# Spreading routing weights over partitions: by matmul or by transfers from memory

## The chip, the cores and the metric

The kernel is written in Bass, by hand, for one core of one Trainium2 chip. Five engines run their own instruction streams side by side and wait for each other by semaphores: TensorE (PE) for matmuls and transposes, VectorE (DVE), ScalarE (ACT), GpSimd (POOL) and SyncE (SP). SP issues nearly all DMA transfers; 16 DMA engines carry them out. The metric is the device time of one execution in microseconds.

## The reference

Two layers work on 8 x 256 tokens of 256 numbers. Each has a norm, an attention, a norm and a set of experts, and each adds its result to x. The change concerns the first set of experts, which is:

```python
scores = sigmoid(x @ router_w.T)                    # 2048 tokens x 16 experts
_, topk_idx = top_k(scores + e_bias, 4)
topk_w = take_along_axis(scores, topk_idx, axis=1)
topk_w = topk_w / (topk_w.sum(axis=1) + 1e-20)
combine = zeros((T, 16)).at[arange(T)[:, None], topk_idx].add(topk_w)
for gu_w, d_w, c in zip(gate_up_proj, down_proj, combine.T):   # 16 experts, 96 hidden each
    g, u = split(x @ gu_w.T, 2, axis=1)
    routed = routed + c[:, None] * (silu(g) * u @ d_w.T)
shared = silu(x @ shared_gate_w.T) * (x @ shared_up_w.T) @ shared_down_w.T
```

All 16 experts are computed for all tokens, and the weight of an expert is zero for a token that did not choose it. The second layer has a cross attention over 64 context rows and 8 experts of 704 hidden rows, of which each token takes two.

## The kernel before

**The first experts as one wide layer.** The 16 experts with 96 hidden rows each stand side by side as 1536 hidden rows, in 12 chunks of 128; a 13th chunk, of 96 rows, is the shared expert. So a chunk holds rows of two experts, and the routing weight must be there per hidden row (partition) and token (column). The 2048 tokens are 16 tiles of 128, in 4 groups of 4 tiles (NG = 4), so that a chunk's hidden values for a group are a tile of 128 x 512.

**One cycle.** For each group `g` and each chunk `c` (0 is the shared one, `chunk_of` gives the place of the others), TensorE does `up0` (gate and up, each 2 halves of the 256 inputs, each as three matmuls of high and low parts: 12 matmuls of 512 columns, into banks 0 to 3 of PSUM) and `down0` (4 tiles of tokens, three matmuls each of 256 columns, into banks 6 and 7). ACT makes silu of the gate (L837). DVE multiplies it with the up half (L1713, "product"), multiplies with the routing weights (L1718), makes the high part (a cast, L1723) and the low part in two halves (a subtraction, L1727, `h_low`), for which `down0` waits. TensorE's order in `ffn0_group` is: `up0` of chunk c+1, then `down0` of chunk c.

**How the weights come to the partitions.** DVE chooses the experts of the first four tiles before the first cycle, and those of the other twelve in pieces in the first group's cycles (`select_rest`). It splits the weights in three bfloat16 parts (`c3`, 96 columns). TensorE turns them (`turn_weights`, L1182), ACT copies them into `cT` (L828), and for each chunk one bfloat16 matmul (L1161) with a matrix of ones and zeros, `spread`, puts the chunk's weights for 512 tokens into bank 4 of PSUM, from which L1718 reads them. GpSimd makes `spread` at the start of the kernel (L544, L548).

**What runs beside it.** GpSimd makes low parts: first of the inputs and of the first experts' weights (L558, L566, L572), then of the second experts' weights. Those, 68 parts of 128 x 512, are loaded by SP (L427), copied to a high part by ACT (L855), subtracted by GpSimd (L604, two instructions a part) and stored again by SP as high and low part (L436, L438). `parts_by` deals them out: 11 in the first group, from its fifth chunk on, and 19 in each later one, that is two in the chunks 2, 4, 6, 8, 10 and 12 and one in the others. ACT handles them behind the cycle's silu. GpSimd waits for the choice of the first four tiles (`pool.wait_ge(b_c3, 3)`) before it goes on with the low parts of the inputs.

In the groups 1 to 3, DVE also makes the statistics of the next norm (chunks 1 and 3) and its rows (chunks 5 and 7, L1472).

## Time and profile before

| | |
|---|---|
| median of 3 runs | 739.35 us (735.06 to 740.98) |
| the profiled execution's own time | 740.54 us |
| its span, first to last instruction | 738.8 us |
| mean granted TensorE clock | 0.941 |
| TensorE busy | 694.2 us, 94% of the span |
| VectorE busy | 471.8 us, 64% |
| ScalarE busy | 257.4 us, 35% |
| GpSimd busy | 356.1 us, 48% |
| moved by DMA | 114.96 MB, mean 156 GB/s |

The profile is of one execution. All times of its rows are in microseconds from the first instruction; "busy" is the time in which at least one instruction of the engine runs. The time outside the span is 1.7 us. A matmul's duration includes the way through the array, so matmuls overlap and their starts tell what each costs.

### The profile page before, as it was taken

The page shows a single profiled execution, that of the slowest core. Times are in us where ns is not written, and L with a number is a line of the kernel's source. Part 1 is how long each engine was busy: PE and PEld are TensorE (multiplying, and loading weights), DVE is VectorE, ACT ScalarE, POOL GpSimd, SP SyncE. Part 2 cuts the span into 40 slices and gives each one's busy share as a digit, 9 for nine tenths or more (in the row PEclk, how much of TensorE's full clock was granted, in tenths as well). Part 3 has the DMA queues.
Part 4 walks back from the last instruction along what each step waited for, and adds up shares of the span by engine and source line. Part 5 has one row for each costly group of instructions (what it writes and reads, how often), then busy time and mean ns, then how long its engine had stood idle before and what let it go on. Part 6 is the DMA issues. An engine that isn't in the chain of part 4 may idle for free.

```text
span 738.8 us, 14867 instructions
## 1 busy us (share of the span) xinstructions
PE 694.2 (94%) x4707; PEld 622.9 (84%) x4707; DVE 471.8 (64%) x1331; ACT 257.4 (35%) x484; POOL 356.1 (48%) x435
## 2 busy tenths in 40 slices
PE   4899999999999999998999984899999999999996
PEld 3758878888888888886677773799999999999995
DVE  4958597677777777775799958344544454454443
ACT  1355512333333333346466622222222232323221
POOL 6217693455446545549222034255354655465553
PEclk9786599999999999999899985899999999999999
DMA  9900103678877787769900047422425445434222
GB/s 220 343 3 1 58 0 122 236 247 271 264 242 257 262 265 248 248 230 430 367 20 31 31 138 267 147 44 41 154 45 151 97 122 155 151 75 135 44 37 22
DMA packets 60266, 114.96 MB, mean 156 GB/s; under 512 B 15185, under 2 KB 29394, under 8 KB 57778
## 3 DMA queue, kind: packets, MB, share of 16 engines
q1 hardware_dynamic: 50514, 103.48, 41.0%
q0 software_dynamic: 8736, 10.39, 8.5%
q8 instruction: 37, 0.61, 0.3%
q10 hardware_dynamic: 960, 0.33, 0.2%
q14 instruction: 19, 0.16, 0.1%
HBM read 68.89 MB, written 45.29 MB: 155 GB/s over the span
## 4 chain that ended last, share of the span: by engine, by line
PE 84%; DVE 10%; issue 3%; ACT 2%; DMA 1%; POOLq 0%; POOL 0%; DVEq 0%
PE ps L1114 19%; PE ps L1115 19%; PE ps L1116 19%; PE ps L1399 4%; PE ps L1244 2%; PE ps L1253 2%; PE ps L986 2%; PE ps L1290 2%; PE ps L1050 2%; PE ps L1041 2%; PE ps L1161 1%; PE ps L1266 1%; PE ps L1201 1%; PE ps L1378 1%; PE ps L1282 1%
## 5 line engine op out<-in xcount | busy, mean ns | idle before, releaser
L604 POOL TENSOR_TENSOR part_lo<-wexp,part_hi 128x256 fp32r<-128x256 f32 x136 | 104.8, 795 | 107.4 <-ACT part_hi L855 106.6
L715 POOL DMA_INDIRECT out_rows<-vbd,slot_row x39 | 63.3, 1623 | 105.6 <-DVE vbd L1947 74.0
L1114 PE MATMUL ps<-w_hi,x_high 128*128 x312 | 104.6, 335 | 1.1 <-DVE x_low L1952 1.1
L1115 PE MATMUL ps<-up_low,x_high 128*128 x312 | 101.1, 324 | 0.0
L1116 PE MATMUL ps<-w_hi,x_low 128*128 x312 | 101.0, 324 | 0.0
L1968 DVE TENSOR_TENSOR arena<-arena,ps 128x704 f32<-128x704 f32 x39 | 34.6, 888 | 102.5 <-ACT arena L954 102.5
L1114 PE MATMUL ps<-xn_high,gu_high 128*128 (+3 forms) x208 | 90.9, 437 | 0.0
L837 ACT ACTIVATE wexp<-ps 128x512 f32<-128x512 f32 (+1 forms) x52 | 31.1, 599 | 147.1 <-PE ps L1116 147.1
L1115 PE MATMUL ps<-xn_low,gu_high 128*128 (+3 forms) x208 | 81.9, 394 | 0.0
L1116 PE MATMUL ps<-xn_high,gu_low 128*128 (+3 forms) x208 | 81.7, 393 | 0.0
L954 ACT ACTIVATE arena<-ps 128x704 f32<-128x704 f32 x39 | 29.6, 760 | 119.1 <-PE ps L1116 119.1
L538 POOL TENSOR_TENSOR rstd<-ve,mhalf 128x2 f32<-128x2 f32 (+1 forms) x31 | 23.3, 751 | 91.7 <-DVE ve L1461 91.7
L1727 DVE TENSOR_TENSOR h_low<-wexp,h_high 128x256 fp32r<-128x256 f32 (+1 forms) x104 | 62.6, 642 | 1.8
L1114 PE MATMUL ps<-dn_high,h_high 128*128 128x256 f32 (+1 forms) x208 | 59.7, 287 | 1.3 <-DVE h_low L1727 1.3
L1114 PEld LDWEIGHTS ps<-w_hi,x_high 128*128 128x128 f32 x312 | 59.3, 190 | 1.5 <-issue 1.5
L1114 PE MATMUL ps<-w_hi,hT_high 128*128 x195 | 58.2, 298 | 2.0 <-DVE hT_high L1961 2.0
L1115 PEld LDWEIGHTS ps<-up_low,x_high 128*128 128x128 f32 x312 | 59.4, 190 | 0.0
L1116 PEld LDWEIGHTS ps<-w_hi,x_low 128*128 128x128 f32 x312 | 59.2, 190 | 0.0
L1115 PE MATMUL ps<-dn_low,h_high 128*128 128x256 f32 (+1 forms) x208 | 58.8, 283 | 0.0
L1116 PE MATMUL ps<-dn_high,h_low 128*128 128x256 f32 (+1 forms) x208 | 58.6, 282 | 0.0
L1116 PE MATMUL ps<-w_hi,hT_low 128*128 x195 | 55.0, 282 | 0.0
L1115 PE MATMUL ps<-down_low,hT_high 128*128 x195 | 55.0, 282 | 0.0
(297 smaller groups left out, 1675.1 us busy)
## 6 DMA issues: line engine op xcount, KB each, us to landing
wexp<-in_wexp SPq DMA_DIRECT2D x68, 256.0 KB, 3.4
w_hi_rows<-part_hi SPq DMA_DIRECT2D x68, 256.0 KB, 3.1
w_lo_rows<-part_lo SPq DMA_DIRECT2D x68, 256.0 KB, 2.7
w_hi<-w_hi_rows SPq DMA_DIRECT2D x8, 2048.0 KB, 19.5
up_low<-w_lo_rows SPq DMA_DIRECT2D x8, 1408.0 KB, 6.0
down_low<-w_lo_rows SPq DMA_DIRECT2D x8, 768.0 KB, 8.3
wexp<-in_gu SPq DMA_DIRECT2D x2, 1632.0 KB, 11.2
xn_rows<-arena SPq DMA_DIRECT2D x8, 256.0 KB, 2.1
```

Of the source, the lines that this page charges most:

```text
L538: pool.tensor_tensor(rstd[:, bass.ds(b * TB, TB)], ve[:, bass.ds(b * TB, TB)], mhalf[:, 0:1].broadcast_to([P, TB]), ALU.pow).then_inc(ln_r ...
L604: r = pool.tensor_tensor(part_lo[:, n % 2, some], part_w[:, n % 4, some], part_hi[:, n % 2, some].bitcast(F32), ALU.subtract)
L715: pool.indirect_dma_start(out=out_rows, out_offset=bass.IndirectOffsetOnAxis(ap=slot_row[:, i:i + 1], axis=0), in_=yb[:, i % 2, :], in_off ...
L837: act.activation(sg0[0:rows, c % 2, :], bank(c % 2)[0:rows, :], ACT.Silu).then_inc(b_silu, 1)
L954: act.activation(sg1.rearrange("p (a n) -> p a n", a=2), bank(0, 2).rearrange("p (a n) -> p a n", a=2)[:, :, 0:HALF1], ACT.Silu).then_inc( ...
L986: mm = pe.transpose(bank(bank_of(norm, k))[:, m * S + j * P:m * S + (j + 1) * P], rows[:, m * P:(m + 1) * P], ident[:, :])
L1114: pe.matmul(out, high, rows_high, start=start, stop=False, skip_group_check=True)
L1115: pe.matmul(out, high, rows_low, start=False, stop=False, skip_group_check=True)
L1116: return pe.matmul(out, low, rows_high, start=False, stop=stop, skip_group_check=True)
L1399: mm = pe.transpose(bank(4, 2)[:, c * P:(c + 1) * P], h1[:, c * P:(c + 1) * P], ident[:, :])
L1727: dve.tensor_tensor(h_low[0:rows_, c % 2, cols], hm0[0:rows_, c % 2, cols], h_high[0:rows_, c % 2, cols].bitcast(F32), ALU.subtract).then_ ...
L1968: dve.tensor_tensor(h1[:, 0:I1].rearrange("p (a n) -> p a n", a=2), sg1.rearrange("p (a n) -> p a n", a=2), bank(2, 2).rearrange("p (a n) ...
```

## The change

The routing weights are no longer spread by TensorE. TensorE turns the float32 weights of a group of tiles (64 rows: 4 tiles x 16 experts) with one transpose per group, ACT copies them, SP stores them into a table in memory (`cw_rows`, 16 experts x 2048 tokens), and for each chunk SP loads the two experts' rows into one of four buffers in SBUF (`w_spread`), each row repeated over its partitions. DVE multiplies with that buffer. The split in three bfloat16 parts, the matrix `spread` and the memset of `c3` go. GpSimd's wait for the choice goes. A few semaphores are merged. The SP queue, which only handled the parts, now runs by group and chunk.

```diff
-        cT = arena[0:96, 0:1024].bitcast(BF16)
-        c3 = arena[:, 1024:1792].bitcast(BF16).rearrange("p (t c) -> p t c", t=NT)
-        spread = arena[0:96, 1792:2560].bitcast(BF16)
+        cT = arena[0:4 * E0, 0:NT // 4 * P]
...
+        w_spread = [view(wexp, at, 512) for at in (20416, 20928, 4096, 4608)]
+        w_in, cw_stored = [sem(f"w_in{n}") for n in range(4)], sem("cw_stored")
+        cw_rows = nc.dram_tensor("cw_rows", (E0, NT * P), F32, kind="Internal").ap()
...
+            def store_weights(first, groups):
+                for j in range(4):
+                    sp.dma_start(cw_v[:, first:first + groups, j, :],
+                                 cT[j * E0:(j + 1) * E0, first * P:(first + groups) * P].rearrange(
+                                     "e (g p) -> e g p", p=P)).then_inc(cw_stored, 16)
+
+            def load_weights(n):
+                g, c = n // (C0 - 1), chunk_of(n % (C0 - 1) + 1)
+                if n >= 4:
+                    sp.wait_ge(b_mult, n - 3)
+                sp.wait_ge(cw_stored, 16 * 8 if g else 16 * 4)
+                e = c * P // I0
+                edge = (e + 1) * I0 - c * P
+                for expert, lo, hi in ((e, 0, edge), (e + 1, edge, P)):
+                    sp.dma_start(w_spread[n % 4][lo:hi, :],
+                                 cw_rows[expert, g * 512:(g + 1) * 512].partition_broadcast(hi - lo)).then_inc(w_in[n % 4], 16)
...
+            sp.wait_ge(b_cT, 1)
+            store_weights(0, 1)
+            sp.wait_ge(x_new, XA)
+            for n in range(3):
+                load_part(n)
+            for n in range(3):
+                load_weights(n)
+            for g in range(NG):
+                for q in range(C0):
+                    if g == 0 and q == 10:
+                        sp.wait_ge(b_cT, 2)
+                        store_weights(1, NG - 1)
+                    n = g * (C0 - 1) + q + 2
+                    if q and n < NG * (C0 - 1):
+                        load_weights(n)
+                    for part in range(parts_by(g, q - 1), parts_by(g, q)):
+                        store_part(part)
...
-            pool.memset(spread, 0.0).then_inc(pool_step, 1)
-            v = spread.rearrange("p (e u) -> p e u", e=E0)
-            for part in range(3):
-                pool.wait_ge(pool_step, 10 + part)
-                pool.affine_select(out=v, in_=v, compare_op=ALU.not_equal, fill=1.0, base=-32 * part,
-                                   pattern=[[-1, E0], [0, I0]], channel_multiplier=1).then_inc(pool_step, 1)
...
-            pool.wait_ge(b_c3, 3)
             for n in range(3, 5):
                 low_rows(n)
...
+            def copy_weights(first, groups):
+                act.wait_ge(b_turned, first + groups)
+                at = slice(first * P, (first + groups) * P)
+                act.activation(cT[:, at], bank(4)[0:4 * E0, at], ACT.Copy).then_inc(b_cT, 1)
+            copy_weights(0, 1)
...
                     act.activation(sg0[0:rows, c % 2, :], bank(c % 2)[0:rows, :], ACT.Silu).then_inc(b_silu, 1)
-                    if k == 0 and c == 0:
-                        copy_weights(0)
                     if k == 0 and c == 9:
-                        copy_weights(1)
-                        copy_weights(2)
-                    if k == 0 and c == 11:
-                        copy_weights(3)
+                        copy_weights(1, NG - 1)
...
-                    if c:
-                        if k == 0 and c == 1:
-                            pe.wait_ge(b_cT, 1)
-                            pe.wait_ge(pool_step, 13)
-                        else:
-                            pe.wait_ge(b_mult, g * (C0 - 1) + c - 1)
-                        pe.matmul(bank(4), spread[:, chunk_of(c) * P:(chunk_of(c) + 1) * P], cT[:, bass.ds(g * 512, 512)],
-                                  start=True, stop=True).then_inc(b_spread, 1)
...
-                for j in range(4):
-                    mm = pe.transpose(at[0:96, j * P:(j + 1) * P], c3[:, 4 * g + j, :], identb[:, :])
-                mm.then_inc(b_turned, 1)
+                pe.wait_ge(b_chosen, 2 if g else 1)
+                pe.transpose(bank(4)[0:4 * E0, g * P:(g + 1) * P], cw0[:, 4 * g:4 * g + 4, :].rearrange("p t e -> p (t e)"),
+                             ident[:, :]).then_inc(b_turned, 1)

             up0(0, 0, 0)
             pe.wait_ge(b_sig, 1)
+            pe.wait_ge(v_ready, B)
+            turn_weights(0)
             ffn0_group(0, 0)
...
                     if c:
-                        dve.wait_ge(b_spread, g * (C0 - 1) + c)
-                        dve.tensor_tensor(hm0[:, c % 2, :], hm0[:, c % 2, :], bank(4), ALU.mult).then_inc(b_mult, 1)
+                        dve.wait_ge(w_in[(c - 1) % 4], g * (32 * (C0 - 1) // 4) + 32 * ((c - 1) // 4 + 1))
+                        dve.tensor_tensor(hm0[:, c % 2, :], hm0[:, c % 2, :], w_spread[(c - 1) % 4], ALU.mult).then_inc(b_mult, 1)
```

Where instructions moved, the two programs' order shows it. First TensorE, between the first chunk's up matmuls (of 96 rows) and the second chunk's; before:

```order
L1114 MATMUL ps<-xn_high,gu_high 96x512
L1115 MATMUL ps<-xn_low,gu_high 96x512
L1116 MATMUL ps<-xn_high,gu_low 96x512
L1114 MATMUL ps<-xn_high,gu_high 128x512
L1115 MATMUL ps<-xn_low,gu_high 128x512
```

and with the change (the three lines of `in_parts` are now L1134 to L1136):

```order
L1134 MATMUL ps<-xn_high,gu_high 96x512
L1135 MATMUL ps<-xn_low,gu_high 96x512
L1136 MATMUL ps<-xn_high,gu_low 96x512
L1186 MATMUL ps<-ident,arena 64x128
L1134 MATMUL ps<-xn_high,gu_high 128x512
L1135 MATMUL ps<-xn_low,gu_high 128x512
```

The transpose of the first weights (L1186), which stood behind the second chunk as four instructions, now stands ahead of it. Next ScalarE, from the sigmoid of the router's scores on; before (L837 is silu, L828 the copy of the turned weights, and a table load belongs to the function behind it):

```order
L824 ACT_TABLE_LOAD
L824 ACTIVATE arena<-ps 128x256
L837 ACT_TABLE_LOAD
L837 ACTIVATE wexp<-ps 96x512
L828 ACTIVATE arena<-ps 96x512
L837 ACTIVATE wexp<-ps 128x512 x5
```

and with the change (L862 is silu, L852 the copy):

```order
L847 ACT_TABLE_LOAD
L847 ACTIVATE arena<-ps 128x256
L852 ACTIVATE arena<-ps 64x128
L862 ACT_TABLE_LOAD
L862 ACTIVATE wexp<-ps 96x512
L862 ACTIVATE wexp<-ps 128x512 x5
```

The copy moved ahead of the first silu and of the load of its table. Last SyncE's queue, behind the first stores of the filler rows; before:

```order
L420 DMA po_rows<-arena 128x8
L427 DMA wexp<-in_wexp 128x512 [waits x_new]
L427 DMA wexp<-in_wexp 128x512 x3
L436 DMA w_hi_rows<-part_hi 128x512 [waits p_hi]
L438 DMA w_lo_rows<-part_lo 128x512 [waits p_lo]
```

and with the change:

```order
L418 DMA po_rows<-arena 128x8
L430 DMA cw_rows<-arena 16x128 [waits b_cT]
L430 DMA cw_rows<-arena 16x128 x3
L425 DMA wexp<-in_wexp 128x512 [waits x_new]
L425 DMA wexp<-in_wexp 128x512 x2
L442 DMA wexp<-cw_rows 96x512 [waits cw_stored]
L442 DMA wexp<-cw_rows 32x512
L442 DMA wexp<-cw_rows 64x512 [waits cw_stored]
```

Four stores into the table and the wait for ACT's copy stand ahead of the first parts, and two loads per chunk (96 and 32 partitions, or 64 and 64) come in between the parts from then on, three chunks ahead of their use.

## Rows read from the trace of the kernel before

**Rows 1.** The page's chain of work that ended last, by engine.

```profile
PE 84%; DVE 10%; issue 3%; ACT 2%; DMA 1%; POOLq 0%; POOL 0%; DVEq 0%
```

**Rows 2.** Busy time by stretch, one group: stretch, length, engines, clock, DMA, GB/s.

```profile
core 0: us, PE busy (x) PEld busy (x) DVE busy (x) ACT busy (x) POOL busy (x), PEclk, DMA share, GB/s
155.00:213.50 58.50, 58.24 (x333) 50.35 (x332) 43.67 (x87) 19.19 (x34) 30.93 (x40) 1.00 0.78 258
```

**Rows 3.** Summaries of single lines: duration ns least/median/most, first and last start.

```profile
L1161 PEld LDWEIGHTS ps<-arena x48: 96/97/98, 97.9 to 323.8; 96*128 96x128 bf16 x48
...
L1718 DVE TENSOR_TENSOR wexp<-wexp,ps x48: 686/689/689, 98.4 to 324.3; 128x512 f32<-128x512 f32 x48
...
L1727 DVE TENSOR_TENSOR h_low<-wexp,h_high x104: 411/426/962, 95.3 to 326.3; 128x256 fp32r<-128x256 f32 x96, 96x256 fp32r<-96x256 f32 x8
```

**Rows 4.** Timeline, TensorE, a spreading matmul and the next: start, length, what.

```profile
206.71 0.39 PE L1161 MATMUL ps<-arena 96*128 x1
206.94 0.47 PE L1114 MATMUL ps<-xn_high,gu_high 128*96 x1
```

**Rows 5.** The start of the kernel: timeline of GpSimd and TensorE, summary of L1499.

```profile
10.29 1.57 POOL L548 TENSOR_SCALAR_AFFINE_SELECT arena<-arena 96x1536 bf16<-96x1536 bf16 x1
...
L1499 DVE TENSOR_SCALAR wexp<-wexp,small x2: 340/870/1399, 10.6 to 11.9; 128x256 f32<-128x256 f32 x2
...
12.42 1.94 PE L997 MATMUL ps<-wexp 128*128 128x64 f32 x8 [4.56 <-DVE wexp L1499]
```

**Rows 6.** Timeline, VectorE, a cycle with two parts (idle before and its releaser in brackets).

```profile
178.79 0.69 DVE L1713 TENSOR_TENSOR wexp<-wexp,ps 128x512 f32<-128x512 f32 x1 [0.68 <-ACT wexp L837]
179.82 0.69 DVE L1718 TENSOR_TENSOR wexp<-wexp,ps 128x512 f32<-128x512 f32 x1 [0.34 <-PE ps L1161]
180.55 0.53 DVE L1723 CAST h_high<-wexp 128x512 fp32r<-128x512 f32 x1
...
181.11 0.84 DVE L1727 TENSOR_TENSOR h_low<-wexp,h_high 128x256 fp32r<-128x256 f32 x1
...
181.87 0.95 DVE L1727 TENSOR_TENSOR h_low<-wexp,h_high 128x256 fp32r<-128x256 f32 x1
```

**Rows 7.** Timeline, GpSimd, three of the four instructions of the same cycle.

```profile
179.36 0.73 POOL L604 TENSOR_TENSOR part_lo<-wexp,part_hi 128x256 fp32r<-128x256 f32 x1 [2.97 <-ACT part_hi L855]
...
180.05 0.74 POOL L604 TENSOR_TENSOR part_lo<-wexp,part_hi 128x256 fp32r<-128x256 f32 x1
...
180.75 0.92 POOL L604 TENSOR_TENSOR part_lo<-wexp,part_hi 128x256 fp32r<-128x256 f32 x1
```

**Rows 8.** Timeline, TensorE, the same chunk's down matmuls, first and second half.

```profile
182.37 0.28 PE L1114 MATMUL ps<-dn_high,h_high 128*128 128x256 f32 x1
...
183.08 0.28 PE L1114 MATMUL ps<-dn_high,h_high 128*128 128x256 f32 x1
```

**Rows 9.** Timeline, an h_low over GpSimd's power of two columns.

```profile
221.65 0.89 POOL L538 TENSOR_TENSOR rstd<-ve,mhalf 128x2 f32<-128x2 f32 x1
...
222.02 0.42 DVE L1727 TENSOR_TENSOR h_low<-wexp,h_high 128x256 fp32r<-128x256 f32 x1
```

**Rows 10.** Timeline, the first microseconds of the first experts, several engines.

```profile
88.97 1.28 ACT L837 ACT_TABLE_LOAD   x1
...
91.56 0.22 DVE L1629 TENSOR_TENSOR arena<-arena,recs 128x64 f32<-128x64 f32 x1
...
92.57 0.40 PE L1116 MATMUL ps<-xn_high,gu_low 128*96 128x512 f32 x1
...
92.84 3.01 POOL L566 TENSOR_TENSOR xn_low<-wexp,xn_high 128x256 fp32r<-128x256 f32 x4 [4.19 <-DVE arena L1658]
...
93.00 0.59 ACT L837 ACTIVATE wexp<-ps 96x512 f32<-96x512 f32 x1 [2.76 <-PE ps L1116]
...
98.44 0.69 DVE L1718 TENSOR_TENSOR wexp<-wexp,ps 128x512 f32<-128x512 f32 x1
```

**Rows 11.** The parts' stores in SP's queue: issue ns, and time to landing.

```profile
L436 SPq DMA_DIRECT2D w_hi_rows<-part_hi x68: 319/320/723, 116.6 to 325.6; - x68
...
DMA to landing us min/median/max: 2.0/3.1/5.5
```

104 lines of the change are left out of this document (32 added, 72 removed).

## The prediction

> **What bounds the kernel now.** I read the chain of work first: TensorE carries 84% of it and VectorE 10% [rows 1]. The table by stretches puts the changed stage in place. In the first experts' stage one group of 512 tokens takes 58.50 us; TensorE is busy in 58.24 of it at the full granted clock, VectorE in 43.67, GpSimd in 30.93, and the DMA engines stand at 0.78 of their time while moving 258 GB/s [rows 2]. So in this stage TensorE sets the end, and VectorE, GpSimd and the DMA engines have slack, but not much. Then the summaries of single lines gave prices [rows 3], and the timelines of single cycles and of the stage's first microseconds showed who waits for whom [rows 4 to 11].
>
> I call one chunk of 128 hidden rows a cycle: 12 matmuls up, 12 down and one spreading matmul.
>
> **The change, step by step.** Times are summed against the profiled execution's own 740.54 us; the median of the three runs is 739.35, 1.19 lower, and I move the result by that at the end.
>
> *1. The spreading matmuls go.* There are 48 [rows 3]. One pushes the next matmul 0.23 us back (206.71 to 206.94) [rows 4]. The first three lie where VectorE, not TensorE, sets the pace (step 4), so 45 count: 45 x 0.23 = -10.4 us. VectorE's wait for them, 0.34 us between the two products of a cycle (179.48 to 179.82) [rows 6], is no gain of its own.
>
> *2. The start of the kernel.* GpSimd no longer makes the spreading matrix. Its last piece runs from 10.29 for 1.57 us, and over it the first of two like VectorE instructions takes 1.40 us, the second 0.34; TensorE begins at 12.42, behind them [rows 5]. TensorE waited for nothing else there, so -1.1 us. If a transfer ends next instead, 0.
>
> *3. The product with the weights moves from PSUM to SBUF.* This is the term I trust least to intuition. The instruction with a PSUM operand takes 686 to 689 ns in all 48 cases, with GpSimd running or not [rows 3]. The instructions with two SBUF inputs (h_low) take 426 ns in the median and up to 962, and the long ones stand over GpSimd's (181.11 with 0.84, over the one from 180.75 to 181.67) [rows 3, 6, 7]. The new product has two SBUF inputs too, w_spread and hm0. Its own length, unheld, no row shows: it lies between 0.43 (256 columns) and 0.85 (twice that), and I keep the 0.69 of the PSUM form with as many columns.
>
> Read off row by row: a VectorE instruction of this kind begins its work 0.14 us before the end of a running GpSimd one (h_low ends at 181.95, 0.42 after 181.53; GpSimd's ends at 181.67), and a GpSimd one that had to wait ends 0.60 after VectorE's end (the cast's at 181.08) [rows 6, 7]. With these two numbers I write out the cycle with two parts, zero being the product's start (178.79). GpSimd's first instruction runs 0.57 to 1.30. The product ends at 0.69; the new one may start at 1.16 and ends at 1.85 (before: 1.72, since it waited 0.34 for TensorE). GpSimd's second ends at 2.45, the cast waits to 2.31 and ends at 2.74 (before 2.29). GpSimd's third ends at 3.34, the first h_low waits to 3.20 and ends at 3.62 (before 3.16); the second ends at about 4.50 (before 4.03). TensorE began the down matmuls at 3.58 and their second half at 4.29 [rows 8]; without the spreading matmul it comes at 3.35 and 4.06. With 0.04 from one engine's end to another's start it waits 0.31, then 0.17 more: 0.48 us, twice what the cycle saves. In a cycle with one part GpSimd has two instructions, and the first h_low ends at 3.20, in time for 3.35, so those cycles keep the whole 0.23.
>
> There are 6 two-part cycles in each of the three later groups and 3 in the first, 21 in all: 21 x 0.48 = +10.1 us. A GpSimd instruction on two columns does not hold VectorE (h_low at 222.02 takes 0.42 over the power from 221.65) [rows 9]; those on 256 columns do. The lower end is 0 (GpSimd off VectorE's instructions); the upper +13.7, if besides the twelve cycles in which VectorE also makes statistics or rows of the next norm lose 0.3 each, a first h_low's wait.
>
> The Trainium skill is stricter, in "SBUF — State Buffer", § Who interferes with whom: of a VectorE instruction with two SBUF inputs and a GpSimd one that reads SBUF, whoever issues second is blocked until the first has finished. With each wait 0.14 us longer for it, and three of them ahead of the first h_low, the term would be about 21 x 0.9 = +19 and the sum +10. The rows show the release 0.14 before the end [rows 6, 7], so the measured number goes into the sum and the rule's case is counted with rival C.
>
> *4. The first weights.* This path is new. Before, the choice's last step kept by the change ends at 91.78, TensorE issues the first chunk's matmuls until 92.8, and transposes and copy come behind the second chunk and the first silu [rows 10]. Now the transpose stands before the second chunk's up matmuls, and ACT copies before its first silu. Three things are late: the choice itself, since GpSimd now runs over it instead of waiting until 92.84 [rows 10], by 0 to 2.5 us (five short instructions with two inputs, up to 0.5 each; I take 1.5); the silu, since its table load (1.28 us, hidden at 88.97 today) [rows 10] now stands behind the copy; and the table's round trip. With the choice at 93.3 the copy ends at 94.1, the table load at 95.4, silu at 96.0, 2.4 later than before (93.59). In that time the four stores issue (0.32 each as the parts' stores, landing from 2.0 later [rows 11]), then the three part loads and the first weights, 0.4 each, landing 3.1 later as a store does in the median: 94.1 + 1.3 + 2.0 + 0.8 + 3.1 = 101.3. VectorE reaches the first such product at 98.44 [rows 10] + 2.4 = 100.8, so the load is the later one: some 2.9 us late. GpSimd is done with its pieces 4.19 us earlier, which frees a VectorE instruction or two of the second and third chunk (0.4 us each). I take +2.5, between +0.5 (choice not slowed, table load hidden) and +5 (all of it, and a landing of 5.5 us).
>
> *5. Edits at nothing.* Sixteen bfloat16 transposes become four of float32 (a few tenths either way). The merged semaphores wait for the same events. The DVE instructions removed in the rest of the choice lay in VectorE's slack of 14 us in 58.5 [rows 2]. The part loads wait for the first copy now, but the parts' first store is at 116.6 us [rows 11].
>
> *6. The queue and the DMA engines.* SP's queue takes two more issues in each cycle (0.64 us at 0.32), ahead of the parts' loads and stores. Traffic in one group: 19 parts of three transfers of 256 KB, 14.9 MB; the weights add 12 x 256 KB = 3.1 MB. At 258 GB/s the share is 0.78, so full use would be 330 GB/s [rows 2]. 18.1 MB in the 55.8 us that TensorE would leave are 324 GB/s, 0.98 of it. I price it at 0, because a late part has most of a cycle before it holds ACT's next silu. If that cover is gone it is rival B.
>
> Sum: -10.4 - 1.1 + 10.1 + 2.5 + 0 = +1.1. 740.54 + 1.1 = 741.6 profiled, 740.4 as a median: no change.
>
> **Rivals.** *A: GpSimd and VectorE do not get in each other's way*, because GpSimd drifts off VectorE's instructions. For it: the product no longer waits 0.34 us; against: the 0.84 and 0.95 [rows 6]. Then term 3 is about 0.5: -10.4 - 1.1 + 0.5 + 2.5 = -8.5, 731 us.
>
> *B: the DMA engines become the bound*, the side on which it is slower. A weight row is read 32 to 96 times from one place in memory, which no transfer of this size in the trace does. If such a load takes twice the time of a plain one, a group needs (14.9 + 6.3) MB at 330 GB/s = 64.2 us, against 58.5 today: +5.7 in each of three groups, +17.1, and in the rest -2.1 (spreading) + 1.4 (contention) - 1.1 + 2.5 = +0.7: 757 us. At 1.4 times it is 58.5 and 740. It decides from about 1.6 times (746.7). For it: share 0.78 already, landings of up to 5.5 us against 2.0 at the least [rows 11]. Against: a row of 2 KB, once read, may be quick to read again.
>
> The Trainium skill gives about 358 GB/s of memory bandwidth for a core ("DMA: Bandwidth & Descriptors", § Specifications); by that 324 GB/s would fit, and rival B would need the repeated reads.
>
> *C: GpSimd's wait was the point.* Choice slowed by 2.5 and every cycle with statistics late as well: the upper ends of terms 3 and 4 together, -11.5 + 13.7 + 5 = +7.2, 746.6 us, the edge of 1%.
>
> **Numbers.** A change under 1% (7.4 us) is about what a measurement of this kernel can't tell from none. The forecast with C: 0.50, its own range 733 to 746.6. A: 0.17. B: 0.33, most of it between 747 and 765. So faster 0.17, same 0.50, slower 0.33, and a range of 729 to 760.
>
> **What would show it.** Right: product rows of the new line at 0.69 where GpSimd rests and about 1.1 where it runs; a group of 57 to 59 us with TensorE waiting for h_low in the two-part cycles; silu first at 95 to 96; TensorE's first matmul behind VectorE at 11.4. Wrong: TensorE never idle and 55.5 us a group (A); ACT or VectorE waiting for transfers, landings over 4.5 us and a DMA share near 1 (B).

## The result, and the profile after

The changed kernel takes 745.16 us in the median of 15 executions (740.95 to 748.9), the kernel before 738.15 us in 15 beside them (731.87 to 740.98). The ratio is 1.0103, with a 95% interval of 1.0073 to 1.0133: slower by about 1%, 7 us. The forecast was 740.4 us in 729 to 760. The time lies in the range, 4.8 us above the value; whether the change is under 1% the interval can't tell, as it holds that bound. Some executions of the kernels edited for the experiments lie 12 us or more above the others of their kernel, so what is compared between profiles is above all groups 1 to 3, where the granted clock is 0.99 to 1.00.

The profiled execution of the changed kernel has a time of 740.95 us, almost that of before (740.54), and still the kernel is 7 us slower. The two differ in TensorE's granted clock ahead of the first experts. These are windows of both kernels (length, busy time with count of TensorE, its weight loads, VectorE, ScalarE and GpSimd, then the granted clock, the DMA share and GB/s); first before:

```profile
61.20:88.40 27.20, 27.20 (x114) 24.47 (x113) 17.48 (x61) 14.85 (x22) 19.93 (x29) 0.50 0.12 39
```

and after:

```profile
61.20:79.20 18.00, 15.58 (x100) 14.03 (x99) 15.28 (x54) 12.71 (x19) 13.79 (x20) 0.81 0.00 0
```

Half the full clock (1.2 instead of 2.4 GHz) stood there for 27 us in the one, and mostly the full clock in the other. Both kernels have executions of both kinds. Of the changed kernel's 15, those at a mean clock of 0.962 and more take 741 to 742 us (6 of 7), those at 0.955 and less 746 to 749; before's take 732 to 733 at 0.966 and more, and mostly 737 to 742 at 0.957 and less. So profiles are comparable only at the same clock. A second profile of the changed kernel (experiment 1) has before's clock there, and the account below uses it. These are four stretches: from TensorE's first matmul to the first experts, the first group (to its first addition to x), groups 1 to 3, the rest; before:

```profile
12.42:88.37 75.95, 72.64 (x311) 59.45 (x311) 55.96 (x294) 37.10 (x77) 34.79 (x50) 0.71 0.35 111
88.37:153.00 64.63, 64.09 (x355) 53.74 (x356) 50.43 (x135) 18.55 (x32) 34.91 (x46) 0.97 0.38 126
153.00:329.09 176.09, 175.30 (x999) 151.55 (x998) 132.28 (x259) 58.91 (x106) 92.11 (x120) 1.00 0.76 252
329.09:738.80 409.71, 380.21 (x3039) 356.58 (x3037) 229.52 (x626) 141.55 (x269) 184.08 (x192) 0.95 0.42 124
```

and after, the second profile:

```profile
11.37:87.31 75.94, 72.73 (x311) 59.52 (x311) 55.26 (x293) 37.07 (x77) 34.80 (x50) 0.71 0.32 100
87.31:154.08 66.77, 62.68 (x331) 52.28 (x332) 51.50 (x126) 16.83 (x29) 35.73 (x45) 0.95 0.60 181
154.08:334.12 180.04, 172.55 (x963) 144.27 (x962) 134.92 (x259) 61.53 (x107) 91.99 (x121) 1.00 0.91 300
334.12:744.98 410.86, 380.69 (x3039) 356.75 (x3037) 229.60 (x626) 141.51 (x269) 184.19 (x193) 0.95 0.43 124
```

TensorE starts 1.05 us earlier, the first group takes 2.14 us more, groups 1 to 3 take 3.95 more, the rest 1.15 more: +6.2 in all. TensorE's busy time in groups 1 to 3 fell by 2.75 us, but the stretch grew: the engine waits. In the first profile of the changed kernel these groups took 181.78, +5.7. At the higher clock the two kernels' times lie some 9 us apart (741 to 742 against 732 to 733); before has no profile there, so this account doesn't cover the difference. In the changed kernel's first profile the first group took 70.81 us against 66.77 in the second.

Who waits is to be seen at ScalarE. These are its waits in groups 1 to 3 (total, times, longest), before:

```profile
ACT wexp L837 <- PE ps L1116: 106.4, 38, 3.8
ACT part_hi L855 <- issue: 1.7, 2, 1.1
```

and after (first profile; L862 is silu, L875 the copy of a part's high part):

```profile
ACT part_hi L875 <- issue: 63.5, 29, 3.9
ACT part_hi L875 <- DMA w_hi_rows<-part_hi: 40.6, 20, 2.7
ACT wexp L862 <- PE ps L1136: 13.4, 9, 3.9
```

ScalarE used to wait for TensorE's up matmuls ahead of each silu. Now it stands for 104 us at the part's copy. The list puts 63.5 us of that down to "issue", but the trace's landing times settle it: in all 49 cases the copy starts 0.07 us after the store from two parts earlier has landed, which frees the buffer that the copy writes (there are two), and its own part's load had landed at least 2.6 us before. The silu behind it is then late. One such place, a cycle with two parts from ScalarE's timeline in the first of the three groups:

```profile
186.65 0.63 ACT L875 ACTIVATE part_hi<-wexp 128x512 fp32r<-128x512 f32 x1 [0.94 <-issue]
189.99 0.63 ACT L875 ACTIVATE part_hi<-wexp 128x512 fp32r<-128x512 f32 x1 [2.70 <-DMA w_hi_rows<-part_hi]
190.53 0.58 ACT L862 ACTIVATE wexp<-ps 128x512 f32<-128x512 f32 x1
```

The transfers themselves land later; median from issue to landing in groups 1 to 3, before and then after:

```profile
w_hi_rows<-part_hi SPq DMA_DIRECT2D x56, 256.0 KB, 3.2
wexp<-in_wexp SPq DMA_DIRECT2D x53, 256.0 KB, 3.5
```

```profile
w_hi_rows<-part_hi SPq DMA_DIRECT2D x57, 256.0 KB, 4.9
wexp<-in_wexp SPq DMA_DIRECT2D x53, 256.0 KB, 5.1
wexp<-cw_rows SPq DMA_DIRECT2D x22, 192.0 KB, 4.4
```

Where the chain of before was 84% TensorE [rows 1], that of after holds transfers:

```profile
PE 56%; DMA 16%; DVE 13%; issue 6%; SPq 4%; ACT 3%; POOL 2%; POOLq 0%; DVEq 0%; ACTq 0%
```

### The profile page after: what moved, and what is told of

It reads as the page before. It is cut to its first block, busy times and chain, and to the rows that moved or that the text cites. A ratio compares the mean times of both kernels' runs of the same rounds, so it can differ in the third digit from the quotient of the medians.

```text
span 739.2 us, 14870 instructions
## 1 busy us (share of the span) xinstructions
PE 681.0 (92%) x4647; PEld 606.6 (82%) x4647; DVE 479.2 (65%) x1322; ACT 258.2 (35%) x482; POOL 354.8 (48%) x431
## 4 chain that ended last, share of the span: by engine, by line
PE 56%; DMA 16%; DVE 13%; issue 6%; SPq 4%; ACT 3%; POOL 2%; POOLq 0%; DVEq 0%; ACTq 0%
DMA w_hi_rows<-part_hi 13%; PE ps L1134 11%; PE ps L1135 11%; PE ps L1136 11%; PE ps L1404 3%; PE ps L1249 2%; PE ps L1258 2%; PE ps L1295 2%; POOL part_lo L627 2%; DVE wexp L1700 2%; SPq L442 1%; SPq L425 1%; PE ps L1206 1%; ACT part_hi L875 1%; PE ps L1383 1%
## 5 line engine op out<-in xcount | busy, mean ns | idle before, releaser
L627 POOL TENSOR_TENSOR part_lo<-wexp,part_hi 128x256 fp32r<-128x256 f32 x136 | 109.0, 823 | 114.9 <-ACT part_hi L875 102.0
L1134 PE MATMUL ps<-w_hi,x_high 128*128 x312 | 104.7, 336 | 1.1 <-DVE x_low L1934 1.1
L1136 PE MATMUL ps<-w_hi,x_low 128*128 x312 | 101.2, 324 | 0.0
L1134 PE MATMUL ps<-xn_high,gu_high 128*128 (+3 forms) x208 | 84.2, 405 | 3.3 <-DVE wexp L1695 3.3
L875 ACT ACTIVATE part_hi<-wexp 128x512 fp32r<-128x512 f32 x68 | 42.7, 630 | 114.3 <-issue 65.1
L1136 PE MATMUL ps<-xn_high,gu_low 128*128 (+3 forms) x208 | 82.1, 394 | 0.0
L1134 PE MATMUL ps<-dn_high,h_high 128*128 128x256 f32 (+1 forms) x208 | 62.9, 302 | 11.5 <-DVE h_low L1709 11.5
L1695 DVE TENSOR_TENSOR wexp<-wexp,ps 128x512 f32<-128x512 f32 (+1 forms) x52 | 35.6, 684 | 43.3 <-ACT wexp L862 43.2
L1134 PEld LDWEIGHTS ps<-w_hi,x_high 128*128 128x128 f32 x312 | 59.4, 190 | 1.5 <-issue 1.5
L1709 DVE TENSOR_TENSOR h_low<-wexp,h_high 128x256 fp32r<-128x256 f32 (+1 forms) x104 | 59.2, 609 | 1.8
L1134 PEld LDWEIGHTS ps<-dn_high,h_high 128*128 128x128 f32 (+1 forms) x208 | 39.8, 192 | 25.0 <-DVE h_low L1709 19.0
L1134 PE MATMUL ps<-w_hi,hT_high 128*128 x195 | 58.2, 298 | 2.0 <-DVE hT_high L1943 2.0
L1136 PEld LDWEIGHTS ps<-w_hi,x_low 128*128 128x128 f32 x312 | 59.3, 190 | 0.0
L1136 PE MATMUL ps<-dn_high,h_low 128*128 128x256 f32 (+1 forms) x208 | 59.2, 285 | 0.0
```

The costliest lines, as they stand in the source:

```text
L627: r = pool.tensor_tensor(part_lo[:, n % 2, some], part_w[:, n % 4, some], part_hi[:, n % 2, some].bitcast(F32), ALU.subtract)
L875: act.activation(part_hi[:, n % 2, :], part_w[:, n % 4, :], ACT.Copy).then_inc(p_hi, 1)
L1134: pe.matmul(out, high, rows_high, start=start, stop=False, skip_group_check=True)
L1136: return pe.matmul(out, low, rows_high, start=False, stop=stop, skip_group_check=True)
L1695: dve.tensor_tensor(hm0[0:rows_, c % 2, :], sg0[0:rows_, c % 2, :], bank(2 + c % 2)[0:rows_, :], ALU.mult).then_inc(b_prod, 1)
L1709: dve.tensor_tensor(h_low[0:rows_, c % 2, cols], hm0[0:rows_, c % 2, cols], h_high[0:rows_, c % 2, cols].bitcast(F32), ALU.subtract).then_ ...
```

## The experiments

The theories: **the transfers** (landings hold ScalarE, as above), **the shared path** (VectorE's product, now with two SBUF inputs, and GpSimd hold each other), and **GpSimd's missing wait**. An edit that leaves the weights out changes what the second layer computes on, so most are judged by the stretches of their profiles, which the table gives for all (us). DMA share, landing and copy waits are those of groups 1 to 3: the landing is the median of the part loads, and the copy waits are the time in all that ScalarE stood at the copies of the high parts.

| | first group | groups 1 to 3 | DMA share | landing | copy waits |
|---|---|---|---|---|---|
| before | 64.63 | 176.09 | 0.76 | 3.5 | 1.7 |
| changed, first profile | 70.81 | 181.78 | 0.89 | 5.1 | 104.1 |
| changed again | 66.77 | 180.04 | 0.91 | 5.1 | 110.2 |
| no loads | 66.77 | 176.74 | 0.77 | 3.6 | 6.7 |
| product from PSUM | 67.48 | 179.53 | 0.90 | 4.9 | 108.4 |
| both | 77.76 | 169.49 | 0.80 | 3.5 | 4.1 |
| plain loads | 68.40 | 171.89 | 0.94 | 4.2 | 65.7 |
| one row repeated, input tensor | 85.06 | 179.50 | 0.88 | 5.1 | 104.3 |
| 8 copies | 86.77 | 183.95 | 0.87 | 4.8 | 106.8 |
| one row a load | 82.59 | 176.91 | 0.77 | 3.2 | 6.5 |
| first product in PSUM | 66.45 | 181.72 | 0.88 | 5.2 | 109.2 |
| wait back | 67.75 | 181.85 | 0.88 | 5.1 | 110.4 |
| candidate | 80.18 | 171.99 | 0.88 | 4.6 | 22.8 |
| second candidate | 66.97 | 169.35 | 0.89 | 4.8 | 60.6 |

### 1. The changed kernel again

> The changed kernel once more, unedited, beside the others on one chip. The 15 times of it so far lie at 741 to 749, none near 758. If the missing wait can shut VectorE out in this kernel too, some execution shows about 17 us more than the others (755 to 765); if it never does in some 10 executions, what was seen belongs to the edited kernels. The two groups of times (741 to 742 and 745 to 749) should show again, with mean clocks of about 0.965 and 0.945, if they come from how long the clock is low ahead of the first experts (10.2 or 30.7 us).

Four executions: 746.71, 746.29, 760.78 and 744.82 us. The low kind of clock showed as expected (0.939 to 0.955; none of the four had the high one). And one execution of the unedited kernel took some 15 us more than the others; experiment 5 says what that probably is. Four executions are fewer than the ten that the expectation asked for.

### 2. Loads or shared path

No loads:

```diff
-                    if q and n < NG * (C0 - 1):
+                    if q and n < 4:
...
-                        dve.wait_ge(w_in[(c - 1) % 4], g * (32 * (C0 - 1) // 4) + 32 * ((c - 1) // 4 + 1))
+                        dve.wait_ge(w_in[(c - 1) % 4], 32)
```

> The changed kernel, but only the first 4 of the 48 weight loads are issued; VectorE multiplies with whatever stands in the four buffers, so the routing weights of all later products are wrong ones. The product's two SBUF inputs, and GpSimd, are unchanged. DMA theory (late landings hold ACT's copy of the high part, and with it the next silu): the DMA share of groups 1 to 3 falls from 0.89 to about 0.8, landings go back to about 3.4 us for the part loads, a group falls from 60.6 us to 56 to 57, the time by some 10 to 13 us, to 732 to 735. Contention theory (VectorE and GpSimd hold each other over the new product): groups stay at 60 or more and the time at 743 or more. The prediction's own sizes (contention 0.48 us in two-part cycles, DMA nothing) would leave the groups where they are too.

Product from PSUM (bank 4 is filled once, by one matmul more):

```diff
+            pe.matmul(bank(4), gu_high[:, 0, 0:P], xn_high[:, 0, 0:512], start=True, stop=True)
...
-                        dve.tensor_tensor(hm0[:, c % 2, :], hm0[:, c % 2, :], w_spread[(c - 1) % 4], ALU.mult).then_inc(b_mult, 1)
+                        dve.tensor_tensor(hm0[:, c % 2, :], hm0[:, c % 2, :], bank(4) if k else w_spread[(c - 1) % 4], ALU.mult).then_inc(b_mult, 1)
```

> The changed kernel with all its loads, but in groups 1 to 3 VectorE multiplies with bank 4 of PSUM as the kernel before did, which here holds other numbers, so the weights are left out of the result; it still waits for each load. One matmul more fills bank 4 at the start (0.23 us). Contention theory: the product is back to 0.69 in every cycle, groups fall from 60.6 to about 57, the time to 734 to 737. DMA theory: groups stay at 60 to 60.5 with the DMA share at 0.89, the time at 743 to 745.

Both edits:

> Both edits together: 4 loads only, and the product from PSUM in groups 1 to 3 (the routing weights are left out of the result). Neither cause is left, so both theories expect TensorE to be the bound again: a group of 58.5 - 12 x 0.23 = 55.7 us, and 3 x 4.9 = 14.7 us off the changed kernel's time, 730 us. If it is longer than 57 us a group, a third cause is there (TensorE waiting for something else).

Measured, groups 1 to 3: 176.74 without loads, 179.53 with the product from PSUM, 169.49 with both. The times were 734.98 to 760.01 (4 executions), 743.51 in the median of 10 and 737.18 of 6; the profiles carry the verdict. From 169.49 on, where neither cause is left, the shared path alone adds 7.25 us and the loads alone 10.0; together they add 10.6 to 12.3, not 17. So neither theory alone holds: without loads its own theory expected 168 to 171 us and the other 180 and more; with the product from PSUM the shared path's theory expected about 171 and the transfers' 180 to 181.5. Both causes are real, and they overlap; that h_low comes late by the longer of the two delays rather than by their sum fits this and isn't shown. Without loads ScalarE waits for TensorE again (98.8 us), and VectorE's new product (groups 1 to 3: shortest/median/longest, ns) shows the shared path at its full size, no loads first, then the changed kernel:

```profile
L1700 DVE TENSOR_TENSOR wexp<-wexp x36: 691/1122/1281, 158.3 to 326.1; 128x512 f32<-128x512 f32 x36
```

```profile
L1700 DVE TENSOR_TENSOR wexp<-wexp x36: 691/816/1136, 155.1 to 327.1; 128x512 f32<-128x512 f32 x36
```

For "both" I expected 55.7 us a group, and over 57 if a third cause was there. It is 56.5, so none is needed.

### 3. What of the loads: the queue, the bytes, the repeated row

One row a load:

```diff
+                    hi = lo + 1 if n >= 4 else hi
                     sp.dma_start(w_spread[n % 4][lo:hi, :],
```

> The changed kernel with all its 96 issues of weight loads and all their waits, but from the fifth product on each moves one row of 2 KB and not 32 to 96 (the other partitions keep old weights, so the result is not the reference's). It parts the bytes from the queue. If the bytes (the DMA engines' time) make the part loads and stores late: groups 1 to 3 together fall from about 181 us to about 176.7, as with no loads, and the part loads land in 3.5 us again. If SP's queue does it (0.8 us of issuing per cycle, and waits on VectorE ahead of the parts' stores): they stay at 180 to 182, with landings near 3.5 us but the parts still late.

Two executions took 755.12 and 752.77 us, the profiled one with the stall of experiment 5. All issues and waits of SP's queue are there and the groups take 176.91 us, as without loads, with ScalarE at the parts' copies for 6.5 us. So it is what the loads move, and not their issues in SP's queue.

Plain rows, and then one repeated row, both from the second experts' weights:

```diff
-                                 cw_rows[expert, g * 512:(g + 1) * 512].partition_broadcast(hi - lo)).then_inc(w_in[n % 4], 16)
+                                 w_flat[lo:hi, n * 512:(n + 1) * 512]).then_inc(w_in[n % 4], 16)
```

> The changed kernel, but each weight load reads as many plain rows of 2 KB of the second experts' weights, one per partition, and not one row repeated over 32 to 96 partitions (so the routing weights are left out of the result). Same number of transfers, same bytes into SBUF. If the repeated read is what makes the loads dear (the prediction's rival B), their landing falls below 4.2 us and the groups from 60.6 to 58 or less. If it is the plain number of bytes and packets, nothing changes: 60 to 61 us a group, the time within 2 us of the changed kernel's; more memory traffic from distinct addresses could even make it a little longer.

```diff
-                                 cw_rows[expert, g * 512:(g + 1) * 512].partition_broadcast(hi - lo)).then_inc(w_in[n % 4], 16)
+                                 w_flat[expert, n * 512:(n + 1) * 512].partition_broadcast(hi - lo)).then_inc(w_in[n % 4], 16)
```

> As the experiment with plain loads, from the same input tensor, but one row repeated over the 32 to 96 partitions, as the changed kernel repeats its table's (so the routing weights are left out of the result). If repeating a row is what delays: groups 1 to 3 together at about 180 to 182 us and landings of 4.2 us, as in the changed kernel. If the tensor's place matters and not the repeating: 171 to 174 us and landings of 3.5 us, as with plain rows.

The pair differs only in whether the partitions read different rows or the same one. Groups 1 to 3 of the plain rows, then of the repeated row:

```profile
147.77:319.66 171.89, 169.35 (x963) 144.76 (x962) 138.34 (x260) 62.99 (x109) 100.02 (x122) 1.00 0.94 314
```

```profile
172.32:351.82 179.50, 172.66 (x963) 144.38 (x962) 135.52 (x259) 61.68 (x107) 93.73 (x120) 1.00 0.88 300
```

and the landings of parts and of weight loads in the same order:

```profile
wexp<-in_wexp SPq DMA_DIRECT2D x54, 256.0 KB, 4.2
wexp<-in_wexp SPq DMA_DIRECT2D x22, 192.0 KB, 3.9
```

```profile
wexp<-in_wexp SPq DMA_DIRECT2D x54, 256.0 KB, 5.1
wexp<-in_wexp SPq DMA_DIRECT2D x22, 192.0 KB, 4.3
```

Repeating the row costs 7.6 us in three groups. It does not cost the engines' time: share times length is 0.94 x 171.89 = 161.6 us for plain rows, 0.88 x 179.50 = 158.0 for the repeated one and 0.89 x 181.78 = 161.8 for the changed kernel, all with 54 MB. What grows is the time until a transfer, and the others beside it, have landed. So bytes as such did not cost either: as many from different rows leave the groups below those without loads. Executions at a clock of 0.963 to 0.964 point the same way: 731.35 and 733.03 us with plain rows, 738.36 with the repeated one (each of the two kernels also had one or two of over 750, experiment 5).

That plain loads (171.89) beat no loads at all (176.74) neither theory expected. VectorE's product is shorter with them (800 against 1122 ns in the median), so the loads seem to shift GpSimd's work off VectorE's; that it is this shift is argued from the durations, not shown.

The Trainium skill ("DMA: Bandwidth & Descriptors", § Latency and other measured facts) gives a memory access 0.2 us on average and 2 us at high load. From before to the changed kernel the trace agrees in direction: part loads land in 5.1 us at a DMA share of 0.89 to 0.91, in 3.5 at 0.76. Between plain and repeated rows it doesn't go by the share: 4.2 us at 0.94 against 5.1 at 0.88. That the load on one place in memory is what does it, no run here shows.

Eight copies of the table, so that neighbouring partitions read different addresses:

```diff
-                    sp.dma_start(w_spread[n % 4][lo:hi, :],
-                                 cw_rows[expert, g * 512:(g + 1) * 512].partition_broadcast(hi - lo)).then_inc(w_in[n % 4], 16)
+                    sp.dma_start(w_spread[n % 4][lo:hi, :],
+                                 cw_rows[:, expert, g * 512:(g + 1) * 512].unsqueeze(0).broadcast_to(
+                                     [(hi - lo) // 8, 8, 512])).then_inc(w_in[n % 4], 16)
...
```

> The changed kernel with the table in memory kept in 8 copies, 132 KB apart (a row of 2048 tokens and 2 KB of padding, 16 of them), and the repeated rows of a load dealt out over the 8 copies, so that neighbouring partitions read different addresses. Bytes and transfers of the loads are the same; only the stores of the table grow (16 of 128 rows of 512 B where 8 of 16 to 48 stood). Repeated-address theory: the loads' median landing falls from 4.25 to about 3.5 us, groups 1 to 3 together from 181.8 to 172 to 174 us, as with plain rows (171.9). If 8 addresses are still too few: somewhere between 174 and 180. Plain-load-of-another-tensor theory (the loads of e4 were fast because of where they read, not because the rows differ): 180 to 182.

The copies are in fact 160 KB apart (16 rows of 10 KB); the 132 KB in the expectation is my slip. Groups 1 to 3 took 183.95 us, the four times were 755.3 to 769.83: no gain. It is inconclusive on the address, because these transfers also took 0.6 to 0.8 us to issue instead of 0.4, and because their outermost dimension has 4 to 12 steps instead of 32 to 96, with an effect that isn't known. Why a repeated row lands late stays open.

### 4. The shared path, for itself

```diff
-                    dve.tensor_tensor(hm0[0:rows_, c % 2, :], sg0[0:rows_, c % 2, :], bank(2 + c % 2)[0:rows_, :],
+                    dve.tensor_tensor(bank(4) if c else hm0[0:rows_, 0, :], sg0[0:rows_, c % 2, :], bank(2 + c % 2)[0:rows_, :],
                                      ALU.mult).then_inc(b_prod, 1)
...
-                        dve.tensor_tensor(hm0[:, c % 2, :], hm0[:, c % 2, :], w_spread[(c - 1) % 4], ALU.mult).then_inc(b_mult, 1)
+                        dve.tensor_tensor(hm0[:, c % 2, :], bank(4), w_spread[(c - 1) % 4], ALU.mult).then_inc(b_mult, 1)
```

> The changed kernel, but VectorE writes its first product (silu times up) to bank 4 of PSUM for the chunks 1 to 12 and the product with the weights reads it there, so this has one SBUF input instead of two; the transposes of the weights go to bank 5. All loads stay. Contention theory: the product falls from 0.82 to 0.69 or so in the median and its longest from 1.18 to under 0.8; groups 1 to 3 together fall from 181.8 to about 179.5, what the product from PSUM gave with all loads. If one SBUF input is enough to be held by GpSimd, the product stays at 0.8 to 1.2 and the groups at 181 to 183.

```profile
L1701 DVE TENSOR_TENSOR wexp<-ps,wexp x36: 691/691/694, 159.2 to 330.6; 128x512 f32<-128x512 f32 x36
```

With one SBUF input the product is never held: 691 ns in the median and 694 at most, with all loads and GpSimd running. Yet groups 1 to 3 stayed at 181.72 us (743.4 us in the median of 4), with ScalarE at its copies for 109.2: what the product gave back was lost in waiting for the silu. The expected 179.5 was wrong by that. The Trainium skill ("SBUF — State Buffer", § Who interferes with whom) says that a VectorE instruction with at most one SBUF input does not contend with GpSimd; the trace agrees, with 694 against 1136 ns.

### 5. GpSimd's missing wait

The profile of "both" took 77.76 us for its first group. The reason is one VectorE instruction, the first of the choice:

```profile
88.10 14.81 DVE L1617 TENSOR_TENSOR arena<-arena,ebias 128x64 f32<-128x64 f32 x1 [3.48 <-ACT arena L847]
```

It adds 128 x 64 numbers with both inputs in SBUF and takes 0.50 us in the changed kernel's first profile. GpSimd meanwhile, in the same execution:

```profile
87.73 2.80 POOL L590 TENSOR_TENSOR xn_low<-wexp,xn_high 128x256 fp32r<-128x256 f32 x4
90.49 2.12 POOL L582 TENSOR_TENSOR gu_low<-wexp,gu_high 128x256 fp32r<-128x256 f32 x3
...
98.70 4.13 POOL L590 TENSOR_TENSOR xn_low<-wexp,xn_high 128x256 fp32r<-128x256 f32 x6
```

22 instructions without a pause from 87.73 to 102.83, and VectorE's ends at 102.91. It got no turn between them: it was shut out until GpSimd had nothing left. The profiles with 8 copies, one row and the repeated row show the same (14.81, 15.22 and 14.79 us; each time it ends 0.09 us behind the last of 22 instructions of GpSimd, as here), and it is most of what makes their first groups 82.6 to 86.8 us long. In the other profiles without the wait the same instruction took 0.42 to 0.50 us over the same row of GpSimd's. In the kernel before it can't last: GpSimd has its own wait there, for the very choice that VectorE is making, and stands from 88.65 to 92.84 [rows 10]. With that wait put back in the changed kernel:

```diff
             gate_low(5)
+            pool.wait_ge(b_chosen, 1)
             for n in range(3, 5):
```

> The changed kernel with GpSimd's wait for the choice put back where it was, ahead of the low parts of the fourth pair of tiles (pool.wait_ge(b_chosen, 1)); nothing else differs. Theory that the missing wait lets GpSimd, which then has some 19 us of work without a pause, shut VectorE out of the choice: no execution with an instruction of VectorE of over 10 us, and no time near 755 to 760; the choice takes 2.8 instead of 3.95 us and the first group about 1 us less. Rival, that the long instruction came from something else (the edits of that experiment): times near 758 turn up here too, and in the unchanged copy sent along none or as many.

Its times were 743.84, 738.8, 749.55 and 738.18 us. The choice took 2.98 us instead of 3.88 in the kernel run again, about as expected, but the first group took 67.75 us and not 66.77 less 1, at the same clock of 0.95 in that stretch, and groups 1 to 3 took 181.85 against 180.04: that miss stays unexplained. At a clock of 0.962 and more, 738.2 and 738.8 stand against six of the changed kernel's at 741 to 742; two executions and a profile that shows no gain don't make these 3 us a finding. None of the 22 executions of the three kernels with the wait was 15 us above the rest of its kernel, and no VectorE instruction in their profiles exceeds 1.3 us. Of the 19 of the changed kernel itself one was (760.78); it was not the profiled one, so that it had this cause is likely and not shown. In the edited kernels without the wait it was 12 or more of 36, by a profile or by a time some 15 us above the others of its kernel. When it strikes and when not isn't known. With one case in 19, the four executions of the changed kernel with the wait can't show that the wait prevents it; with it GpSimd has no such row of work over the choice, and that is the argument.

The same page and section of the Trainium skill call the shared path "an exclusive lock" and name a VectorE instruction with two SBUF inputs as one that contends with a GpSimd one that reads SBUF. The trace shows more: VectorE was blocked over 22 instructions of GpSimd, not over one.

### 6. A version that beats both

The parts' traffic is what the loads collide with, so the candidate moves parts to the first group, and takes up what the other experiments gave: the wait back, the first product in PSUM, silu's table loaded ahead of the copy.

```diff
-PARTS0 = 11
+PARTS0 = 17
...
+            act.preload_act_table(ACT.Silu)
             copy_weights(0, 1)
```

> The changed kernel with four edits: GpSimd's wait for the choice put back; the first product written to bank 4 of PSUM, so that the product with the weights has one SBUF input; ScalarE's table for silu loaded ahead of the copy of the turned weights; and 17 parts of the second experts' weights in the first group and 17 in each later one, where it was 11 and 19, so that a later group moves 13.4 MB of parts and 3.1 MB of weights (of 330 GB/s: 50 us of a group). DMA theory: the share of groups 1 to 3 falls to about 0.85, ACT waits less for stores to land, groups 1 to 3 together come to 172 to 176 us, the first group 1 to 2 us longer than the changed kernel's, the time 6 to 9 us under the changed kernel's, 733 to 738 as a median, and no execution above 750. If the parts' traffic is not what holds ACT: 180 to 182 us for the three groups and a time of 740 to 743, that of the kernel with the wait alone.

Groups 1 to 3 took 171.99 us, as expected (the lower end), but the first group 80.18 instead of 67 to 69, and the time was 747.88 us (ratio to before 1.0162, 1.0105 to 1.0219) and up to 752.78, where 733 to 738 and none above 750 was expected. The last two cycles of its first group took 9.7 and 9.5 us, from silu to silu (L864), behind copies (L877) that waited for the stores to free their buffers. SP had issued nothing from 148.05 to 151.07, behind the stores of the second part of the table, so the store that the first copy needed went out only at 152.36:

```profile
149.41 0.58 ACT L864 ACTIVATE wexp<-ps 128x512 f32<-128x512 f32 x1
156.27 0.63 ACT L877 ACTIVATE part_hi<-wexp 128x512 fp32r<-128x512 f32 x1 [6.29 <-issue]
158.53 0.63 ACT L877 ACTIVATE part_hi<-wexp 128x512 fp32r<-128x512 f32 x1 [1.63 <-DMA w_hi_rows<-part_hi]
159.07 0.58 ACT L864 ACTIVATE wexp<-ps 128x512 f32<-128x512 f32 x1
```

So the first group was mended, in parts, queue and order:

```diff
-PARTS0 = 17
+PARTS0 = 14
...
-                return max(c - 4, 0) * PARTS0 // 8
+                return max(c - 3, 0) * PARTS0 // 9
...
-            for n in range(3):
-                load_part(n)
-            for n in range(3):
-                load_weights(n)
+            for n in range(3):
+                load_weights(n)
+            for n in range(3):
+                load_part(n)
...
-                    if g == 0 and q == 10:
+                    if g == 0 and q == 9:
...
-                    if k == 0 and c == 9:
+                    if k == 0 and c == 8:
                         copy_weights(1, NG - 1)
...
-                    if k == 0 and c == 8:
+                    if k == 0 and c == 7:
                         for later in range(1, NG):
```

> The last candidate again with its first group mended: 14 parts in the first group, from its fourth chunk on (so at most two a chunk, mostly one or two in turn) and 18 in each later one; the first weight loads ahead of the first part loads in SP's queue; the weights of the later groups turned, copied and stored one chunk earlier, so that the first load of the second group does not stop the queue until the table has landed. If the 13 us that the last candidate lost in its first group came from 17 parts in eight chunks (two parts and the weights in 4.2 us are 1.83 MB, 436 GB/s) and from that stop in the queue: the first group falls from 80.2 us to 64 to 66, each of its last chunks to under 5 us; groups 1 to 3 together 173 to 177 us (DMA share 0.88); the start 1.06 us under the kernel before's. In all -1.1 - 0 - 1 = 2 us under the kernel before at equal clock, 734 to 738 in the median: not to be told from it in time, but 7 to 9 us under the changed kernel. Rival, that GpSimd or VectorE and not the transfers held the first group: its first group stays above 70 us.

It takes 733.19 us in the median of 12 (728.01 to 736.22), the kernel before 738.48 of 17 on the same chip: 0.9935, interval 0.9897 to 0.9974, and 0.9935/1.0103 = 0.983 of the changed kernel's. This is faster than before, if by less than 1%. (Expected were 734 to 738.) Its stretches, with before's clock ahead of them:

```profile
87.34:154.31 66.97, 63.11 (x331) 52.13 (x332) 48.10 (x127) 18.43 (x32) 38.09 (x51) 0.95 0.70 224
154.31:323.66 169.35, 167.91 (x963) 145.84 (x962) 126.17 (x259) 59.59 (x104) 86.60 (x114) 1.00 0.89 303
```

Groups 1 to 3 are 6.7 us shorter than before's, TensorE is busy in 167.91 of 169.35; I had expected 173 to 177, and 64 to 66 for the first group, which took 66.97. Part loads still land in 4.8 us, and ScalarE still stands at the copies for 60.6 us: late landings as such cost nothing.

What they cost depends on whether the two buffers of the high part keep up over a whole group. From the start of its copy to the landing of its store, a part holds its buffer for 6.1 us in the mean in the changed kernel (4.2 in the kernel before, 5.5 with plain loads, 5.7 here). As an estimate from these means, 19 parts on two buffers need 9.5 x 6.1 = 58 us of a group that takes 60, so they have next to no slack; before they needed 9.5 x 4.2 = 40 of 58.7, with plain loads 52 of 57.3, and 18 parts here 9 x 5.7 = 51 of 56.5. Neither the first product in PSUM alone (181.72 us) nor the wait alone (181.85) shortened groups 1 to 3, so the step from 19 to 18 parts is what is left to explain the 12 us. It was not run by itself: whether 18 parts are enough with the held product too, and what each edit carries in the first group, is open.

## Why the prediction was right or wrong

By its own steps, at before's clock:

- *Step 2, the start*: -1.1 forecast, -1.05 measured (first matmul at 11.37 for 12.42, experiment 1). Right, in every profile to 0.25 us.
- *Steps 1 and 3 in groups 1 to 3*: 36 x 0.23 = -8.3 and 18 x 0.48 = +8.6, together +0.4; without loads +0.65 (176.74 to 176.09). Right as a sum. Apart they are -6.6 (both edits, 169.49) and +7.25, each about 1.5 us smaller than forecast, and it is luck that the two errors cancel. The product's length was forecast at 0.69 and about 1.1 where GpSimd runs; it is 691 ns at the least and 1122 in the median without loads.
- *Step 4, the first weights*: the first group was forecast at 1.9 us more (-2.1 for nine spreading matmuls, +1.4 for three two-part cycles, +2.5), measured +2.14. The first silu ended at 94.42 and the first product with weights began at 100.35, each after a start 1.06 us earlier: 95.5 and 101.4 in before's time, forecast 96.0 and 101.3. The choice was slowed by 1.1 us and not by the 1.5 assumed. The stretch's mean clock was 0.95 and not 0.97, and in it ScalarE also waited 4.91 us for a store that stood behind the table's stores in SP's queue, which step 4 left out: that the sum fits is in part luck. Missed, though: that GpSimd without its wait can shut VectorE out for 15 us. Rival C had the choice slowed by 2.5 us at most, because the release was read as coming at the end of one GpSimd instruction, and nothing in the rows said that VectorE gets it.
- *Step 6, the queue and the DMA engines*: the term that failed. Priced at 0, it costs 3.3 us (180.04 to 176.74), or 5.0 by the first profile. The sentence that failed is that a late part has most of a cycle before it holds ScalarE's next silu. The high part has two buffers, and a two-part cycle uses both. A buffer needs its copy (0.63 us) and its store's landing: 0.63 + 3.2 = 3.8 us before, under the cycle of about 4.5; 0.63 + 4.9 = 5.5 with the weight loads, over it, so that ScalarE waits. Over a group the two buffers were taken for 58 of 60 us (experiment 6), and that leaves no slack. I compared bytes with the engines' rate, which fits (share 0.89 to 0.91), and not the landing with the buffers. With as many bytes from different rows the groups are shorter than without loads, so it is for repeated rows that 0 was wrong.
- *Rival B* named the repeated reads, rightly, and had the wrong mechanism and so the wrong price. A repeated row takes no more of the engines' time, so 757 us was far off; it lands later, and makes its neighbours land later. Its signs came: landings over 4.5 us, ScalarE waiting for transfers.
- *The rest*, priced at nothing, took 1.15 us more in that profile. Over the profiles it varies by as much (407.0 to 412.0 us between the groups' end and the last instruction); no cause in the change was found.

Sum at equal clock: forecast +1.1, measured +6.2; of the 5.1 missing 3.6 lie in groups 1 to 3 (3.3 of it step 6), 1.15 in the rest, 0.3 in the first group. That the profiled 740.95 meets the forecast of 741.6 is luck of the clock.

## What to carry to other kernels

Where a transfer sits in a small ring of buffers, compare buffer time (work on it plus issue-to-landing, at the traffic after the change), times the parts per buffer, with the stage's length, not only bytes with bandwidth: landings were 1.6 us longer with the repeated rows (share 0.9) than without (0.76), but 0.7 longer with plain rows at 0.94. Here 58 us of buffer time in a group of 60 cost time, and 52 of 57 did not, though ScalarE waited in both. Ask of every removed wait whose turn it protected: GpSimd working without a pause can shut out a VectorE instruction with two SBUF inputs, and one PSUM operand takes it out of that fight. Compare profiles by stretches of equal clock before reading a difference out of them.

## What the hardware showed that I had not expected

- One VectorE instruction of normally 0.42 to 0.50 us took 14.79 to 15.22 us in four profiles, until GpSimd's row of 22 instructions had ended.
- 2 KB rows read by 32 to 96 partitions from one place: same engine time (158 to 162 us in three groups), part loads landing in 5.1 us instead of 4.2 with different rows, 7.6 us in 180.
- The same program is granted full clock ahead of the first experts in some executions and half in others, worth 8 us there (first experts at 79.38 or 87.31 us).
- Plain loads on top of the parts made groups 1 to 3 shorter than no loads (171.89 against 176.74 us).
